# A one-hot as a comparison of two tensors, in the first node stage of a graph and mixture-of-experts kernel

## The reference, cut to what matters

```python
x = x + _L0_gnn_ref(_layernorm(x), edge_index, W_l, W_r, att, bias)
x = x + _L0_ffn_ref(_layernorm(x)[None], Wr, br, W1, b1, W2, b2)[0]

def _L0_ffn_ref(x, Wr, br, W1, b1, W2, b2):      # E = 8, H = 32, TOP_K = 1
    router_logits = xf @ Wr + br
    topk_logits, topk_idx = jax.lax.top_k(router_logits, 1)
    topk_gates = jax.nn.softmax(topk_logits, axis=1)
    for e in range(E):
        h = jax.nn.relu(xf @ W1[e] + b1[e])
        oe = h @ W2[e] + b2[e]
        out = out + jnp.where((idx_k == e)[:, None], gate_k * oe, 0.0)
```

## Time and profile before

| | us |
|---|---|
| median of 3 runs | 2961.64 |
| lowest and highest of them | 2958.59, 2968.72 |
| the profiled execution, its own time | 2959.94 |
| its span in the profile | 2958.2 |

### The profile page before, as it was taken

One profiled execution on the slowest core, in us unless ns is written; L12 is line 12 of the kernel. 1 busy time (PEld: TensorE's weight loads), 2 busy tenths in 40 slices (PEclk: granted clock), 3 DMA queues, 4 the chain that ended last, 5 costly groups with the idle time before them and its releaser, 6 DMA issues. The chain is left out here.

```text
span 2958.2 us, 43948 instructions
## 1 busy us (share of the span) xinstructions
PE 2207.9 (75%) x11789; PEld 1296.0 (44%) x11789; DVE 1857.0 (63%) x5128; ACT 921.4 (31%) x2016; POOL 1774.6 (60%) x2143
## 2 busy tenths in 40 slices
PE   8999999757777728888878859999994477774000
PEld 3444444335554525555543426666663344442000
DVE  5777767534444469999951115777775377776666
ACT  1111111034544414666663315555553000000000
POOL 4555555566666256666526633777777465563776
PEclk9999999969999959999989979999997698997555
DMA  6655555368888545777649966666662599995999
GB/s 204 224 185 184 190 179 193 136 202 262 253 253 263 190 154 182 235 238 242 211 171 332 364 230 203 212 214 215 211 206 69 164 378 356 356 341 193 344 371 339
DMA packets 361398, 698.60 MB, mean 236 GB/s; under 512 B 51609, under 2 KB 85235, under 8 KB 361153
## 3 DMA queue, kind: packets, MB, share of 16 engines
q1 hardware_dynamic: 239672, 399.69, 39.6%
q0 software_dynamic: 76720, 217.93, 23.4%
q10 hardware_dynamic: 44761, 78.17, 7.4%
HBM read 426.08 MB, written 287.17 MB: 241 GB/s over the span
## 5 line engine op out<-in xcount | busy, mean ns | idle before, releaser
L2085 POOL DMA_INDIRECT xg<-n_rows,ids x219 | 219.0, 1000 | 146.5 <-PE psum L154 55.4
L148 PE MATMUL psum<-wl,xT 128*128 128x512 f32 x632 | 288.8, 600 | 0.0
L148 PE MATMUL psum<-wg,yT 128*128 128x512 f32 x632 | 286.0, 595 | 0.0
L148 PE MATMUL psum<-wr,xT 128*128 128x512 f32 x632 | 284.1, 592 | 0.0
L2235 POOL DMA_INDIRECT q<-slot_outputs,qs x158 | 175.3, 1109 | 86.6 <-issue 47.8
L337 ACT ACTIVATE xb<-xa,xsc 128x512 f32<-128x512 f32 x79 | 64.2, 814 | 480.5 <-POOL xsc L397 480.5
L148 PE MATMUL psum<-wc,x1T 128*128 128x264 f32 x632 | 162.4, 401 | 67.0 <-DVE hb L1218 46.5
L1637 POOL DMA_INDIRECT slot_tokens<-sl x158 | 171.0, 1082 | 65.4 <-issue 59.8
L384 POOL TENSOR_TENSOR ve<-mv,epst 128x1 f32<-128x1 f32 x79 | 51.1, 647 | 254.2 <-DVE mv L439 254.2
L1059 POOL TENSOR_TENSOR oc<-ta,ts 128x512 f32<-128x512 f32 x79 | 132.8, 1681 | 113.4 <-DVE ta L1183 63.2
L2173 DVE COPY gT<-psum 128x512 f32<-128x512 f32 x219 | 142.4, 686 | 88.3 <-PE psum L154 46.0
(11 more groups left out here) (320 smaller groups left out, 5545.7 us busy)
## 6 DMA issues: line engine op xcount, KB each, us to landing
slot_outputs<-yo ACTq DMA_DIRECT2D x54, 1024.0 KB
x_rows<-x SPq DMA_DIRECT2D x158, 256.0 KB
edge_sums<-eo SPq DMA_DIRECT2D x29, 1056.0 KB
edge_sums<-go SPq DMA_DIRECT2D x29, 1024.0 KB
xT<-in_xTt SPq DMA_DIRECT2D x79, 256.0 KB
xl_rows<-xl SPq DMA_DIRECT2D x79, 256.0 KB
xr_rows<-xr SPq DMA_DIRECT2D x79, 256.0 KB
residual_rows<-xb SPq DMA_DIRECT2D x79, 256.0 KB
```

The source lines that it names most:

```text
L148: last = nc.tensor.matmul(ps, lhs[:, k, :], rhs[:, k, :], start=(k == 0), stop=(k == DK - 1))
L2085: pool.indirect_dma_start(xg[:, t % 8, :], None, XN3, bass.IndirectOffsetOnAxis(ids[:, t:t + 1], 0), bounds_check=NP - 1, oob_is_err=False ...
```

## The change

`one_hot` compares `iota3` with `ix` as a second tensor, repeated over the 128 elements, where before `ix` was given as one number a partition to the form with a tensor and a number. The values are the same.

```diff
                     dve.wait_ge(c_ix, t + 1)
-                    nc.vector.tensor_scalar(hm[:, h, FC:FC + P], iota3[:], ix[:, h, :], None,
+                    nc.vector.tensor_tensor(hm[:, h, FC:FC + P], iota3[:], ix[:, h, :].to_broadcast([P, P]),
                                             ALU.is_equal).then_inc(c_oh, 1)
```

## The result

| | before | after |
|---|---|---|
| median | 2965.18 us (4 runs) | 2940.2 us (4 runs) |
| lowest and highest | 2958.59, 2970.58 | 2925.61, 2943.63 |
| ratio, 95% interval | | 0.9891 (0.9865 to 0.9917) |
| the profiled execution | 2959.94 us | 2943.63 us |
| the stage of the change, in it | 481.6 us | 448.0 us |

The kernel became faster by 1.1% (the ratio); on 2965 us that is some 32 us, while the two medians of four runs lie 25 us apart. The forecast was 2967.1 us, and the range from 2951 to 2976 us does not hold the result. Rival A1, to which the prediction gave 0.14, is what happened.

What follows compares the result with a forecast made beforehand. VectorE was taken to bound the first node stage. 69 held one-hots at 0.08 us more each gave +5.5 us on the profiled 2959.94, so 2965.4; with 1.7 us up to the median, 2967.1 us, range 2951 to 2976 us.

Steps and rivals of the forecast that it cites:

- A1: Rival: one-hot gets past the waiting add in all 69 held tiles, gaining 40.6 us, to 2921.0 us; chance 0.14.
- What bounds the stage: First node stage: VectorE busy 360.00 of 360.00 us; floor under a gain is TensorE, one one-hot every 4.48 us.
- The count of 69 held one-hots: Old one-hots held until GpSimd's add ends: 66 between 1120 and 1480 us, two before, two behind; 69 of 79 in all.
- the first three: `ts`, `df` and `x` in the stage's first tiles: two-input instructions held beside GpSimd's add for 1.75, 1.63 and 1.35 us.
- A: Rival: one-hot goes ahead of GpSimd's waiting add, as `weight_sum` does; 0.54 us gained an ordinary tile; chances 0.14 and 0.12.
- A2: Rival: one-hot gets past the add only behind `weight_sum`, 16 tiles; gain 7.8 us, to 2953.8 us; chance 0.12.
- Price of a held one: New one-hot beside the add: VectorE goes on 0.09 us behind it, against 0.01; 0.08 us more, 69 times, +5.5 us.
- Price of a free one: Ten one-hots not held: 0.28 us for 128 elements against 0.27 to 0.29 us now; taken as 0.
- The tile under A: Ordinary tile: `routed` is held and lets VectorE go on at 1.63 us, against 2.17 us today.
- B: Rival: two tensors are not held at all; TensorE's floor caps the gain at 67 us, 2895 us; chance 0.05.
- C: Rival: held one-hot starts its work only when the add ends, next start 0.20 us behind; +13.1 us, 2974.7 us; chance 0.10.
- D: Rival: the new form is the old one in disguise; ruled out by TENSOR_TENSOR in all 79 places, no chance given.

## Why the prediction was wrong

**What bounds the stage: right.** VectorE is busy throughout before and after, and TensorE's floor exists (402.9 us without the add). In the second profile of the changed kernel the stage is 35.0 us shorter than in the one before and the execution 36.6 us; in the first it is 33.6 against 16.3, for the last two stages differed. The count of 69 held one-hots in the kernel before was right as well.

**"The new one-hot has both inputs in SBUF, so I take it as held like the first three": this step failed.** The three instructions of the earlier trace rows were held, and the prediction carried that over to the one-hot: a hold of all 69 was to be paid, with 0.08 us more each. Instead three were held. The others took their free length, and the add came to lie beside `x2` and to hold `routed`. The prediction looked at which operands an instruction has, and not at what stands in front of it and whether it is ready. The pair of runs that wait for the last tile's `xq` and for this tile's shows what decides for the one-hot: 445.6 us and no one-hot held, 486.4 us and 69 held. In nearly all tiles, what stands ready right behind a two-input instruction goes ahead of the waiting add; what has to wait for that instruction's completion comes too late.

The three held rows are not one case. `x` at 1107.39 does not stand behind `xq` but behind `hb`, which has one input in PSUM; the add was already at work, as in the runs with `x2` in front. Earlier `x` rows do stand right behind their own `xq` and wait for its completion (line 1211 needs it). They start 0.72 us behind it and are held, as the one-hot is in the run with that wait:

```profile
1091.25 0.69 DVE L1199 SCALAR_TENSOR_TENSOR xq<-oc,xx 128x512 f32<-128x512 f32 x1
1091.48 1.58 POOL L1059 TENSOR_TENSOR oc<-ta,ts 128x512 f32<-128x512 f32 x1 [1.49 <-DVE ta L1183]
1091.97 1.63 DVE L1211 SCALAR_TENSOR_TENSOR x<-mi,xq 128x512 f32<-128x512 f32 x1
```

`ts` at 1078.32 goes against the account. It starts 0.60 us behind `ta` (1077.72), so the trace shows nothing that kept it, and is held all the same by an add that came 0.22 us before. `df` starts at 1080.70, even 0.28 us before the row of the add that it is held beside. And in the first tiles `weight_sum` is held right behind `xq`, twice in the kernel before and at the same two places in both profiles of the changed kernel:

```profile
1087.03 0.68 DVE L1199 SCALAR_TENSOR_TENSOR xq<-oc,xx 128x512 f32<-128x512 f32 x1
1087.13 1.70 POOL L1059 TENSOR_TENSOR oc<-ta,ts 128x512 f32<-128x512 f32 x1 [0.46 <-issue]
1087.63 1.25 DVE L1156 SCALAR_TENSOR_TENSOR rd<-fe,rd 128x32 f32<-128x32 f32 x1
```

So standing ready is what the runs show for the flow of most tiles, and not a full account: what holds these in the first tiles stays open.

**The weighing of A: the evidence was read, and put last.** The earlier trace rows already showed `weight_sum` going ahead of the add, and the prediction counted 16 such tiles. It set three held ones against them, one of them shown, and read a threshold in the add's start into that one, 0.54 against 0.55 us. The changed kernel shows no such threshold. The one-hot of 1453.87 was free with the add 0.45 us ahead; this one was held at the same distance:

```profile
1432.39 1.66 POOL L1059 TENSOR_TENSOR oc<-ta,ts 128x512 f32<-128x512 f32 x1 [0.66 <-DVE ts L1190]
1432.84 1.35 DVE L1241 TENSOR_TENSOR hm<-iota,ix 128x128 f32<-128x128 f32 x1
```

What makes these exceptions stays open. They are three of the 58 one-hots that meet an add in one profile, one of 58 in the next, and seven of 60 in the changed kernel with `routed` moved. Sixteen against three, two of them in the first tiles, should have made A1 and A2 together the likeliest case, not 0.26.

The Trainium skill (SBUF — State Buffer, Who interferes with whom) lets the engine that issues first have the shared ports. The add starts 0.45 us ahead of the one-hot and gets them behind it in 55 of 58 tiles, so the trace does not agree; the three held ones do. The same section exempts the form with an accumulator from the waiting of a tensor with a number; there the run with a sum agrees, with 0.34 us against 1.29.

**The sizes were right.** *Price of a held one:* where 69 two-tensor one-hots are held (the wait on this tile's `xq`), VectorE goes on 0.07 us behind the add in the median and with the old form 0.01. That is 0.07 us more a tile, where the prediction had 0.08, and the stage gives +4.8 us, where the sum had +5.5. *Price of a free one:* 278 and 280 ns without the add, so 0. *The tile under A:* 1.62 us against 1.63. *A1 as a whole* had 40.6 us and the stage gave 33.6. Most of the gap is in one tile of four, in the flow that repeats every four tiles (from the add's start at 1302.01 to that of the add four tiles later at 1322.09, 20.08 us; A1 gives the 22.1 us of before, from 1301.50 to `xq` at 1323.61, less 3 x 0.54 and 0.75, which is 19.7). There GpSimd's fetch keeps the add back:

```profile
1170.78 1.34 POOL L1050 DMA_INDIRECT ai<-edge_sums,nodeq  x1 [0.19 <-issue]
...
1171.69 0.28 DVE L1241 TENSOR_TENSOR hm<-iota,ix 128x128 f32<-128x128 f32 x1
1171.89 0.68 DVE L1260 SCALAR_TENSOR_TENSOR x<-psum,x 128x512 f32<-128x512 f32 x1
1172.15 1.28 POOL L1059 TENSOR_TENSOR oc<-ta,ts 128x512 f32<-128x512 f32 x1
...
1172.50 1.23 DVE L1247 SCALAR_TENSOR_TENSOR hm<-hb,hm 128x256 f32<-128x256 f32 x1
```

The add begins 0.26 us behind `x2`'s start, and `routed` takes 1.23 us instead of 0.88. That is 0.35 us in each four tiles. "GpSimd waits for VectorE's `ts` before each add" was true of the kernel before; with shorter tiles GpSimd's own list is in the way now and then.

**The other rivals.** B is out: beside an add at work the two-tensor one-hot is held (the run with `x2` in front). C is out: a held two-tensor one-hot lets VectorE go on 0.07 to 0.08 us behind the add, not 0.20. D was out from the start.

## What to carry to other kernels

Where an instruction of VectorE is several times longer than its shape asks for and ends with one of GpSimd, don't ask first for a cheaper form: ask what can stand beside GpSimd's instruction (one input in PSUM, or a form with a sum along the row), and put that there. When two engines take turns, look at whether the next instruction stands ready behind the one in work or has to wait for it; a single wait of that kind cost 41 us here (445.6 to 486.4). Then count the exceptions, for some stay. And sixteen rows of the steady flow outweigh one exception in it, however well a threshold could be drawn between them.

## What the runs showed of the hardware that was not expected

- A two-input instruction of VectorE that stands ready right behind another one mostly goes ahead of a GpSimd add that has been waiting for 0.45 us: of 58 one-hots that met an add, 55 went ahead in the profile after, and all 58 in that with one more fulfilled wait, but 53 of 60 with `routed` moved. In the first tiles some are held every time (`weight_sum` at 1087.63 and 1102.75 of the kernel before, and at the same places in the changed one). The form with a tensor and a number was held in the same place 69 times of the 70 that it met an add.
- The form with a sum along the row (335 ns and 78 ns for the read, 0.26 us start to start) is not held beside the add at all. Nor does it hold the add, which ends 1.22 us behind the point at which `xq` is through, as it does in the kernel before.
- A constant fill on GpSimd holds next to nothing: with it the old form had 278 ns as its median and 451 ns as its longest.
